# RWKV attention and a routed expert layer in one kernel: products on ScalarE, adds on POOL, routing one step sooner

## The chip, the cores and the metric

The kernel runs on one core of a Trainium2 chip. A core has five engines that run their own instruction streams and meet at semaphores: TensorE (PE in the profile; PEld is its weight load), VectorE (DVE), ScalarE (ACT), GpSimd (POOL), and SyncE (SP), which here only starts transfers. They work on SBUF, 128 partitions of on-chip memory, and PE writes to PSUM, from which the others read. The metric is the device time of one execution in microseconds. The kernel before takes 846.95 us, the median of 3 runs (845.86 to 848.41).

## What is computed

Two layers on x of 4 sequences of 1024 tokens with 256 channels, each added to x. First, on the normalized x, an RWKV attention with 16 heads:

```python
xx = jnp.pad(x, ((0, 0), (1, 0), (0, 0)))[:, :Tv] - x
xk, xv, xr, xg = x + xx*time_maa_k, x + xx*time_maa_v, x + xx*time_maa_r, x + xx*time_maa_g
r, k, v = xr @ Wr.T, xk @ Wk.T, xv @ Wv.T          # per head
g = gelu(xg @ Wg.T)
att = rc @ kc                                      # per chunk of the sequence
yc = att * Wmat @ vc + rc @ state * wb
new_state = ws * state + kc * wk @ vc
yn = (y - mean) / sqrt(var + EPS) * ln_w + ln_b    # per head
out = yn * g @ Wo.T
```

Then, on the normalized result, a layer of 8 experts: each token picks its two likeliest, and each expert takes at most 320 tokens of a sequence, in their order. A token's place comes from a running count:

```python
count_fused = jnp.cumsum(mask_fused, axis=1)
trunc_mask = expert_mask * (count <= capacity)
expert_out = einsum(silu(h1) * h3, w2)             # h1 = dispatch @ w1, h3 = dispatch @ w3
final = einsum('ebcm,bsec->bsm', expert_out, combine_mask)
```

## The kernel before

Phase one (`phase_a`) does the attention and the routing, in 16 blocks of 256 tokens (two tiles of 128; a sequence is four blocks), all in float32. Phase two (`phase_b`) runs the eight experts and isn't touched. Phase one ends with the first part of expert 0 (`early_...`), for which the rows of the first three sequences are enough.

The order on each engine is written out by hand, as a loop over steps c in which each function gets its own block: the same step works on block c+3's statistics, c+1's projections, c's attention, c-1's output, c-2's and c-3's routing. No scheduler moves anything. An engine waits at the first instruction whose semaphore is not up, and all behind it waits too.

In a step PE does, in this order: `scores_a` (L1317), `across` (L1345), `turn1` (L1290, the transposes of normalized x), `project_g`, `outer` (L1308), four `within` of the first tile, `scores_b`, `project_r`, `project_k`, `across`, four `within` of the second tile (L1354, each waits for one mask of DVE), `count(c-3)` (L1401, L1402), `project_o(c-1)` (L1378), `logits` (L1391), `turn_k` (L1298), `group_sums` (L1368), `project_v` (L1275).

The four mixed inputs come from one difference, `diff` (L964 on DVE): inputs 0, 1 and 2 by `mixing` on DVE (L973: product and sum in one instruction, for two halves of the channels), input 3 by `mixed_g` on POOL (two products at L586, one add at L588).

The routing of a block is `logit_sum`, `logit_max` and `stats2` on DVE, `norm2` on POOL (its last result is `nbias`), `logit_exp` on ACT (L745), `best_two` and `tally` on DVE (L1073 to L1093: the two experts and the running sums), `count` on PE, `slots` on DVE (L1100 to L1114: the row number in each expert's list) and `scatter` on POOL (L610: four indirect transfers that write the tokens' rows). `count` writes into the same PSUM bank that `scores_a` uses next; so `scores_a` waits for `slots`.

ACT turns PSUM into SBUF (`turned1` L793, `receptance` L695, `key`, `value`), does the gate (`gate` L806, gT), z (`scaled` L815), the two norms (`normed1` L764, `normed2` L687) and the high part of expert 0's weights (`weight_high` L785), whose low part is formed on POOL (`weight_low` L594). zg, which `project_o` takes, is z times gT on POOL (`gated` L622). The high and low parts need the raw weights, which SP loads with `first_weights` behind the output of blocks 1, 3 and 8.

Of the kernel before, what the change touches and what calls it, by code (L numbers as in the profile page):

```python
# [23 lines left out]
ALU = mybir.AluOpType  # L24
# [265 lines left out]
def phase_a(nc, sb, ps, ctx, sem, ident, x, maa, decay_row, decay_ch, u_row, weights, lnw, lnb, gateT, disp, out,  # L290
# [117 lines left out]
    diff_ready = sem("diff_ready")  # L408
    mixed_ready = [sem(f"mixed_ready{k}") for k in range(4)]
# [49 lines left out]
    def on_sync(sp):  # L459
# [33 lines left out]
        for b in range(STEPS):  # L493
# [4 lines left out]
            if b in (1, 3, 8):  # L498
                first_weights((1, 3, 8).index(b))
# [8 lines left out]
    def on_gpsimd(pool):  # L508
# [70 lines left out]
        def mixed_g(b):  # L579
            if 0 <= b < STEPS:  # L580
                pool.wait_ge(diff_ready, b + 1)
                if b == 0:
                    pool.wait_ge(maa_in, 16)
                wait(pool, proj_done[3], b)
                for k in range(KT):
                    chain.add(nc.gpsimd.tensor_scalar(mixed[3][:, k, :], diff[:, k, :], maa_sb[:, 3, k:k + 1], None, ALU.mult))  # L586
                chain.sync()
                nc.gpsimd.tensor_tensor(mixed[3][:], mixed[3][:], xT[b % 2][:, :, 1:], ALU.add).then_inc(mixed_ready[3], 1)  # L588
# [39 lines left out]
        for c in range(-3, TAIL):  # L628
            norm2(c - 2)
            mixed_g(c + 1)  # L630
            gated(c - 1)
            if c < TAIL - 1:
                scatter(c - 4, range(0, 1))
# [3 lines left out]
            if c < TAIL - 1:  # L637
                scatter(c - 4, range(1, TPS))
            weight_low(c - 6)
            if c >= TAIL - 2:  # L640
                scatter(c - 3)
# [8 lines left out]
        weight_low(9)  # L650
        scatter(12)
        chain.reset()
        norm2(14)
        gated(15)
# [4 lines left out]
        weight_low(11)  # L659
# [5 lines left out]
    def on_scalar(act):  # L665
# [10 lines left out]
        def decay_tables():  # L676
# [3 lines left out]
            nc.scalar.activation(sdecay[:], lam_ch[:], ACT.Exp, scale=-float(Q)).then_inc(set_act, 1)  # L680

# [150 lines left out]
        for c in range(-2, TAIL):  # L832
            group_log(c - 1)
            value(c)
            if c == 0:
                folded()
            turned1(c + 1)
# [3 lines left out]
            normed1(c + 2)  # L841
            scaled(c - 1)
            normed2(c - 2)
# [8 lines left out]
            weight_high(c - 4)  # L852
            keep_y(c)
            column(c + 1)
            keep_logits(c + 1)

# [21 lines left out]
        weight_high(11)  # L878
        early_hidden_hi(2)
        early_gate(3)  # L880
        early_hidden_hi(3)
        logit_exp(15)
        early_gate(4)
        normed2(15)
# [6 lines left out]
    def on_vector(dve):  # L891
# [64 lines left out]
        def shifted(b):  # L956
            if 0 <= b < STEPS:
# [3 lines left out]
                wait(dve, mixed_ready[3], b)  # L961
# [173 lines left out]
        for c in range(-3, TAIL):  # L1135
# [8 lines left out]
            mask(c, 1, 2)  # L1144
            mask(c, 1, 3)
            state_b(c)
            stats1(c + 3)
            if c == -3:
                center_gate()
            mixing(c + 1, 2)  # L1150
# [1013 lines left out]
```

## Time and profile before

| what | us |
| --- | --- |
| median of 3 runs (range) | 846.95 (845.86 to 848.41) |
| the profiled execution | 846.3 |
| its span, first to last instruction | 844.6 |
| PE busy in the span | 814.7 (96%) |
| DVE busy | 505.7 (60%) |
| ACT busy | 464.4 (55%) |
| POOL busy | 468.3 (55%) |
| granted clock of PE, mean | 0.995 of full speed |

The profile comes from one execution. The shares are means over two phases with different limits, so they are read by stretches. In the timeline a line is one instruction or a run of like ones: start, duration to the end of the last, engine, line and operation, what is written and read, how many; in brackets the idle time of the engine before it and what ended it. The ends of matmuls are modelled, and PE's durations overlap; so PE's work is read from one start to the next. A name like L1378 is the line of the kernel before.

### The profile page before, as it was taken

How to read it: one execution, taken by the hardware profiler on the slowest of the kernel's cores; microseconds unless marked ns; L12 is line 12 of the kernel's file. 1: busy time of each engine (PE TensorE's matmuls, PEld its weight loads, DVE VectorE, ACT ScalarE, POOL GpSimd, SP SyncE). 2: the span in 40 equal slices, each digit the busy share in tenths (PEclk: the TensorE clock that was granted, in tenths of full speed). 3: DMA queues.
4: the chain of work that ended last, by engine and by line, in shares of the span. 5: the costliest groups of instructions: out<-in, count | busy, mean ns of one | idle time of the engine just before them, and what ended most of it. 6: DMA issues, size and time to landing. Idle time of an engine off the chain costs nothing. (4 is left out here: it accounts for less than half of the span.)

```text
span 844.6 us, 17509 instructions
## 1 busy us (share of the span) xinstructions
PE 814.7 (96%) x6291; PEld 674.5 (80%) x6291; DVE 505.7 (60%) x1286; ACT 464.4 (55%) x860; POOL 468.3 (55%) x529
## 2 busy tenths in 40 slices
PE   5999999999999989899999999999999999999997
PEld 4777787777777667678998788898788899788886
DVE  6789988899998886343543543544443545353441
ACT  4478877778787667264543543644552544453331
POOL 6445577777777857475444356453436452535215
PEclk9999999999999999999999999999999999999999
DMA  5852032213111121546333334342415442413114
GB/s 163 334 209 70 28 108 68 76 52 96 40 40 48 58 91 72 178 157 135 101 70 40 110 95 70 95 113 27 124 60 79 121 106 26 95 35 44 20 14 50
DMA packets 50746, 74.30 MB, mean 88 GB/s; under 512 B 5072, under 2 KB 42448, under 8 KB 50640
## 3 DMA queue, kind: packets, MB, share of 16 engines
q1 hardware_dynamic: 35760, 53.72, 19.2%
q0 software_dynamic: 14592, 19.18, 13.6%
q8 instruction: 64, 1.05, 0.5%
q14 instruction: 42, 0.34, 0.1%
q10 hardware_dynamic: 288, 0.01, 0.0%
HBM read 38.67 MB, written 34.22 MB: 86 GB/s over the span
## 5 line engine op out<-in xcount | busy, mean ns | idle before, releaser
L1648 POOL DMA_INDIRECT out<-ysb,index x80 | 124.7, 1558 | 145.6 <-DVE ysb L1887 111.1
L2001 PE MATMUL p<-xh,whi 128*128 128x512 f32 (+2 forms) x504 | 185.4, 368 | 1.4 <-POOL wlo L1637 0.5
L1863 DVE TENSOR_TENSOR hid<-gated,p 128x512 f32<-128x512 f32 (+1 forms) x126 | 81.0, 643 | 176.2 <-ACT gated L1710 176.2
L2003 PE MATMUL p<-xh,wlo 128*128 128x512 f32 (+2 forms) x504 | 185.3, 368 | 0.0
L2002 PE MATMUL p<-xl,whi 128*128 128x512 f32 (+2 forms) x504 | 184.6, 366 | 0.0
L2027 PE MATMUL py<-w,hh 128*128 128x512 f32 x448 | 162.5, 403 | 4.2 <-DVE hl L1132 3.7
L1710 ACT ACTIVATE gated<-p 128x512 f32<-128x512 f32 (+1 forms) x126 | 70.8, 562 | 157.4 <-PE p L2003 152.8
L1637 POOL TENSOR_TENSOR wlo<-wraw,whi 128x448 fp32r<-128x448 f32 x56 | 70.8, 1267 | 89.8 <-ACT whi L1696 84.4
L2001 PEld LDWEIGHTS p<-xh,whi 128*128 128x128 f32 x504 | 94.7, 188 | 19.2 <-issue 3.5
L2026 PE MATMUL py<-w,hl 128*128 128x256 f32 x384 | 108.5, 283 | 0.0
L2002 PEld LDWEIGHTS p<-xl,whi 128*128 128x128 f32 x504 | 94.8, 188 | 15.2
L2003 PEld LDWEIGHTS p<-xh,wlo 128*128 128x128 f32 x504 | 94.7, 188 | 14.7
L2027 PEld LDWEIGHTS py<-w,hh 128*128 128x128 f32 x448 | 83.2, 190 | 19.7 <-DVE hl L1132 4.1
L1737 ACT ACTIVATE ysb<-py,weight 128x256 f32<-128x256 f32 x64 | 30.4, 474 | 111.9 <-PE py L2027 90.0
L1871 DVE TENSOR_TENSOR hl<-hid,hh 128x512 fp32r<-128x512 f32 (+1 forms) x126 | 88.9, 706 | 3.8 <-ACT hh L1719 3.3
L1887 DVE SCALAR_TENSOR_TENSOR ysb<-py,weight,ysb 128x256 f32<-128x256 f32 x64 | 30.9, 483 | 99.8 <-ACT ysb L1737 99.8
L992 DVE TENSOR_TENSOR attm<-pS,dmask 128x512 f32<-128x512 f32 x128 | 79.3, 679 | 7.4 <-PE pS L1317 7.0
L610 POOL DMA_INDIRECT disp<-row,slot_i x64 | 65.6, 1025 | 32.4 <-issue 12.0
L2026 PEld LDWEIGHTS py<-w,hl 128*128 128x128 f32 x384 | 72.8, 190 | 2.9
L1719 ACT CAST hh<-hid 128x512 fp32r<-128x512 f32 (+1 forms) x126 | 72.8, 578 | 1.2 <-DVE hid L1863 1.2
L1250 PE MATMUL pB<-mixed,w_in_sb 128*128 128x256 f32 x256 | 61.3, 383 | 0.2 <-ACT gT L806 0.2
L586 POOL TENSOR_SCALAR mixed<-diff,maa_sb 128x256 f32<-128x256 f32 x32 | 37.9, 1192 | 32.3 <-DVE diff L964 32.3
(215 smaller groups left out, 1430.7 us busy)
## 6 DMA issues: line engine op xcount, KB each, us to landing
wraw<-in_w SPq DMA_DIRECT2D x24, 896.0 KB
disp<-wraw SPq DMA_DIRECT2D x16, 662.5 KB, 8.2
xtok<-disp SPq DMA_DIRECT2D x16, 530.0 KB, 4.8
x_ring<-in_x SPq DMA_DIRECT2D x16, 256.0 KB, 3.3
out<-x SPq DMA_DIRECT2D x16, 256.0 KB
xtok<-disp SPq DMA_DIRECT2D x8, 265.0 KB
out<-ysb,index POOLq DMA_INDIRECT x80
disp<-row,slot_i POOLq DMA_INDIRECT x64
```

The costliest lines, as they stand in the source:

```text
L992: nc.vector.tensor_tensor(attm[g][:], pS[:, :, g // 2, g % 2, :], group_mask(g), ALU.mult).then_inc(attm_ready[g], 1)
L1637: nc.gpsimd.tensor_tensor(to.piece(1, m, q), raw_piece(wraw[k], m, q), to.piece(0, m, q).bitcast(F32), ALU.subtract).then_inc(wlo_ready, 1)
L1648: nc.gpsimd.indirect_dma_start(out, bass.IndirectOffsetOnAxis(ap=index[e.const % 2][:, t:t + 1], axis=0), ysb[j % NY][:], None, compute_op ...
L1710: nc.scalar.activation(gated[k][:, 0:w], p1[k][:, 0:w], ACT.Silu).then_inc(gated_ready, 1)
L1719: nc.scalar.copy(hh[(u * NCH + q) % 2][:, f, 0:w], hid[k][:, 0:w]).then_inc(hh_ready, 1)
L1863: nc.vector.tensor_tensor(hid[k][:, 0:w], gated[k][:, 0:w], p3[k][:, 0:w], ALU.mult).then_inc(hid_ready, 1)
L1871: nc.vector.tensor_tensor(hl[s][:, f, 0:w], hid[k][:, 0:w], hh[s][:, f, 0:w].bitcast(F32), ALU.subtract).then_inc(hl_ready, 1)
L2001: nc.tensor.matmul(dst[:, 0:w], hi[m][:, wcut], xh[xcut], start=(kt == 0), stop=False)
L2002: nc.tensor.matmul(dst[:, 0:w], hi[m][:, wcut], xl[xcut], start=False, stop=False)
L2003: ins = nc.tensor.matmul(dst[:, 0:w], lo[m][:, wcut], xh[xcut], start=False, stop=(kt == KT - 1))
L2026: nc.tensor.matmul(to[:, 0:C], b, w2[:, f, 0, :], start=False, stop=False)
L2027: ins = nc.tensor.matmul(to[:], a, w2[:, f].rearrange("p h c -> p (h c)"), start=(f == 0), stop=(f == FT - 1))
```

## The change

- Inputs 2 and 3 are no longer formed by DVE and by POOL alone. ACT forms the products (`mixed_part`: two activations of 128x256 with a scale for each input), and POOL adds x (`mixed_add`).
- A block's routing after `logit_exp` comes one step sooner: `count(c-2)`, `slots(c-2)`, `scatter(c-3)`. `count` stands behind `project_o` on PE, `best_two` and `tally` before `residual` on DVE, `slots` behind `decayed_k`. `stats1` moves behind `stats2`.
- On ACT `normed2` and `normed1` move to the end of the step, `weight_high` comes one step sooner and stands before `turned1`; `weight_low` too comes one step sooner. SP's third weight load goes behind block 7 instead of 8.
- At the end of phase one block 12's `count`, `slots` and `scatter` are gone, the last zg is formed on DVE (`gated_last`), and the last `logit_exp` stands before `early_gate(3)` on ACT.

```diff
         for b in range(STEPS):
...
-            if b in (1, 3, 8):
-                first_weights((1, 3, 8).index(b))
+            if b in (1, 3, 7):
+                first_weights((1, 3, 7).index(b))
...
-        def mixed_g(b):
-            if 0 <= b < STEPS:
-                pool.wait_ge(diff_ready, b + 1)
-                if b == 0:
-                    pool.wait_ge(maa_in, 16)
-                wait(pool, proj_done[3], b)
-                for k in range(KT):
-                    chain.add(nc.gpsimd.tensor_scalar(mixed[3][:, k, :], diff[:, k, :], maa_sb[:, 3, k:k + 1], None, ALU.mult))
-                chain.sync()
-                nc.gpsimd.tensor_tensor(mixed[3][:], mixed[3][:], xT[b % 2][:, :, 1:], ALU.add).then_inc(mixed_ready[3], 1)
+        def mixed_add(b, k):
+            if 0 <= b < STEPS:
+                pool.wait_ge(part_ready[k], b + 1)
+                nc.gpsimd.tensor_tensor(mixed[k][:], mixed[k][:], xT[b % 2][:, :, 1:], ALU.add).then_inc(mixed_ready[k], 1)
...
+        def mixed_part(b, k):
+            if 0 <= b < STEPS:
+                act.wait_ge(diff_ready, b + 1)
+                wait(act, proj_done[k], b)
+                if b == 0:
+                    act.wait_ge(maa_in, 16)
+                for c in range(KT):
+                    ins = nc.scalar.activation(mixed[k][:, c, :], diff[:, c, :], ACT.Copy, scale=maa_sb[:, k, c:c + 1])
+                ins.then_inc(part_ready[k], 1)
...
             value(c)
             if c == 0:
                 folded()
+            weight_high(c - 3)
             turned1(c + 1)
             group_rstd(c - 1)
             logit_exp(c - 2)
             gate(c)
-            normed1(c + 2)
+            mixed_part(c + 1, 2)
+            mixed_part(c + 1, 3)
             scaled(c - 1)
-            normed2(c - 2)
...
             square_y(c)
-            weight_high(c - 4)
             keep_y(c)
             column(c + 1)
+            normed2(c - 2)
             keep_logits(c + 1)
+            normed1(c + 2)
...
+        def gated_last(b):
+            dve.wait_ge(z_ready, b + 1)
+            dve.wait_ge(gT_ready, b + 1)
+            wait(dve, wo_done, b)
+            nc.vector.tensor_tensor(zg[:], z[:], gT[b % 2][:], ALU.mult).then_inc(zg_ready, 1)
...
-                wait(pe, slot_ready, b - 3)
+                wait(pe, slot_ready, b - 2)
...
-            count(c - 3)
             project_o(c - 1)
+            count(c - 2)
```

On POOL the step reads so before (nbias is the end of `norm2`, disp<-row is `scatter`):

```order
L567 TENSOR_TENSOR nbias<-nlmax,rstd 128x2
L586 TENSOR_SCALAR mixed<-diff,maa_sb 128x256 x2
L588 TENSOR_TENSOR mixed<-mixed,xT 128x512
L622 TENSOR_TENSOR zg<-z,gT 128x512
L605 COPY row<-tok 128x2
L610 DMA disp<-row,slot_i 10240x265 x2
L575 TENSOR_TENSOR r_dec<-rT,rdecay 128x512
L610 DMA disp<-row,slot_i 10240x265 x2
```

and so now, in a step with a piece of the weights (the lines are those of the changed kernel):

```order
L568 TENSOR_TENSOR nbias<-nlmax,rstd 128x2
L600 COPY row<-tok 128x2
L605 DMA disp<-row,slot_i 10240x265 x2
L583 TENSOR_TENSOR mixed<-mixed,xT 128x512
L617 TENSOR_TENSOR zg<-z,gT 128x512
L583 TENSOR_TENSOR mixed<-mixed,xT 128x512
L576 TENSOR_TENSOR r_dec<-rT,rdecay 128x512
L605 DMA disp<-row,slot_i 10240x265 x2
L589 TENSOR_TENSOR wlo_0<-wraw,whi_0 128x448
```

The two products are gone, a second add has come, and three operations of 512 elements follow one another between the two pairs of scatters.

On DVE, from the second tile's masks (attm) on, the step reads so before:

```order
L992 TENSOR_TENSOR attm<-pS,dmask 128x512 x4
L1020 SCALAR_TENSOR_TENSOR state<-state,sdecay,kvm 128x32 x2
L950 BN_STATS st<-x_ring 128x6 x2
L953 BN_AGGR mv<-st 128x2 x2
L973 SCALAR_TENSOR_TENSOR mixed<-diff,maa_sb,xT 128x256 x2
L1037 TENSOR_TENSOR x_0<-x_ring,pX 128x256
L1037 TENSOR_TENSOR x_0<-x_ring,pS 128x256
L1047 SCALAR_TENSOR_TENSOR logit<-xg,std_all,pX 128x8
L1047 SCALAR_TENSOR_TENSOR logit<-xg,std_all,pS 128x8
L1100 TENSOR_TENSOR over<-pS,limit 128x16
```

and so now:

```order
L994 TENSOR_TENSOR attm<-pS,dmask 128x512 x4
L1022 SCALAR_TENSOR_TENSOR state<-state,sdecay,kvm 128x32 x2
L1081 TENSOR_REDUCE lsum<-lexp 128x2
L1082 RECIPROCAL lrec<-lsum 128x2
L1083 TENSOR_TENSOR row<-lexp,lrec 128x2x8
L1085 MAX two<-row 128x8 x2
L1087 MEMSET two 128x2x6
L1089 MATCH_REPLACE mark<-two,row 128x8 x2
L1092 TENSOR_SCALAR took<-mark 128x16
L1098 TENSOR_TENSOR before<-before,took 128x8
L1101 TENSOR_TENSOR before<-before,took 128x8
L1045 TENSOR_TENSOR x_0<-x_ring,pX 128x256
```

`best_two` and `tally` (lsum to the second before) now stand between the state's update and `residual` (x_0<-x_ring), where `stats1` and the mix of input 2 stood.

## Rows read from the trace of the kernel before

**Rows 1.** By stretch: its width, busy us (xcount) PE, PEld, DVE, ACT, POOL; PEclk, DMA, GB/s.
```profile
60.00:280.00 220.00, 218.11 (x2686) 171.61 (x2686) 198.12 (x643) 170.13 (x298) 157.84 (x230) 1.00 0.19 63
```

**Rows 2.** Timeline of PE (start us, duration us, engine, line, operation, count): `turn1`.
```profile
59.80 0.66 PE L1290 MATMUL pX<-ident,xn 128*128 128x128 f32 x4
...
77.39 0.66 PE L1290 MATMUL pX<-ident,xn 128*128 128x128 f32 x4
...
95.41 0.66 PE L1290 MATMUL pX<-ident,xn 128*128 128x128 f32 x4
...
187.54 0.66 PE L1290 MATMUL pX<-ident,xn 128*128 128x128 f32 x4
...
279.82 0.66 PE L1290 MATMUL pX<-ident,xn 128*128 128x128 f32 x4
```

**Rows 3.** Timeline of PE: `project_o` and `logits` of one step, `count` of a later one.
```profile
69.73 1.16 PE L1378 MATMUL pX<-w_o,zg 128*128 128x264 f32 x4
...
71.61 0.95 PE L1391 MATMUL pS<-gate_sb,xT 128*128 128x8 f32 x8
...
197.76 0.40 PE L1401 MATMUL pS<-before,ones 128*128 128x16 f32 x2
```

**Rows 4.** Timeline of DVE: first masks of one step, and pieces of a later one.
```profile
59.37 2.48 DVE L992 TENSOR_TENSOR attm<-pS,dmask 128x512 f32<-128x512 f32 x4 [2.40 <-PE pS L1317]
...
193.71 1.24 DVE L1008 SCALAR_TENSOR_TENSOR state<-state,sdecay,kvm 128x32 f32<-128x32 f32 x2
194.88 2.47 DVE L992 TENSOR_TENSOR attm<-pS,dmask 128x512 f32<-128x512 f32 x4
...
197.59 0.74 DVE L950 BATCH_NORM_STATS2 st<-x_ring 128x6 f32<-128x256 f32 x2
...
198.53 0.89 DVE L973 SCALAR_TENSOR_TENSOR mixed<-diff,maa_sb,xT 128x256 f32<-128x256 f32 x2
200.36 0.42 DVE L1037 TENSOR_TENSOR x<-x_ring,pX 128x256 f32<-128x256 f32 x1 [0.94 <-PE pS L1378]
...
203.89 0.16 DVE L1073 TENSOR_REDUCE lsum<-lexp 128x2 f32<-128x16 f32 x1
...
206.17 0.17 DVE L1093 TENSOR_TENSOR before<-before,took 128x8 f32<-128x8 f32 x1
```

**Rows 5.** Timeline of ACT in the same step.
```profile
194.12 1.08 ACT L815 ACTIVATE z<-yn,lnb_sb,lnw_sb 128x256 f32<-128x256 f32 x2
...
196.55 1.26 ACT L704 ACTIVATE r_pair<-pA,parity 128x512 f32<-128x512 f32 x2
```

**Rows 6.** Timeline of POOL in the same step.
```profile
195.28 1.27 POOL L622 TENSOR_TENSOR zg<-z,gT 128x512 f32<-128x512 f32 x1 [0.54 <-ACT z L815]
...
199.95 1.30 POOL L575 TENSOR_TENSOR r_dec<-rT,rdecay 128x512 f32<-128x512 f32 x1
...
203.72 1.15 POOL L594 TENSOR_TENSOR wlo<-wraw,whi 128x448 fp32r<-128x448 f32 x1
```

**Rows 7.** Timeline of DVE: L1075 alone, and beside POOL's L594.
```profile
74.87 0.18 DVE L1075 TENSOR_TENSOR row<-lexp,lrec 128x16 f32<-128x16 f32 x1
...
204.28 0.63 DVE L1075 TENSOR_TENSOR row<-lexp,lrec 128x16 f32<-128x16 f32 x1
```

**Rows 8.** Timeline: first weight's load, ACT's `turned1`; the stretch 79 to 80 us.
```profile
73.53 0.51 SPq L490 DMA_DIRECT2D wraw<-in_w  x1
...
78.08 0.59 ACT L793 COPY xT<-pX 128x512 f32<-128x512 f32 x1 [1.65 <-PE pX L1290]
...
79.00:80.00 1.00, 1.00 (x38) 0.64 (x38) 0.95 (x3) 0.99 (x2) 0.00 (x0) 1.00 0.06 25
```

**Rows 9.** Timeline of PE near the end of phase one: first instructions after waits.
```profile
313.79 1.10 PE L1368 MATMUL pX<-ysq,blockdiag 128*128 128x256 f32 x4 [1.00 <-DVE logit L1047]
...
321.44 1.16 PE L1378 MATMUL pX<-w_o,zg 128*128 128x264 f32 x4 [0.52 <-POOL zg L622]
...
336.07 0.40 PE L1401 MATMUL pS<-before,ones 128*128 128x24 f32 x2 [0.51 <-DVE before L1093]
```

More of the change, by code:

```diff
@@ L408, in phase_a @@
     diff_ready = sem("diff_ready")
+    part_ready = {k: sem(f"part_ready{k}") for k in (2, 3)}
     mixed_ready = [sem(f"mixed_ready{k}") for k in range(4)]
@@ L629, in on_gpsimd @@
             norm2(c - 2)
-            mixed_g(c + 1)
+            scatter(c - 3, range(0, 1))
+            mixed_add(c + 1, 2)
             gated(c - 1)
-            if c < TAIL - 1:
-                scatter(c - 4, range(0, 1))
+            mixed_add(c + 1, 3)
             decayed_r(c + 1)
@@ L636, in on_gpsimd @@
                 empty_rows()
[L637 to L641, printed above, removed]
+            scatter(c - 3, range(1, TPS))
+            weight_low(c - 5)
+            if c == TAIL - 1:
+                scatter(c - 2)
             norm1(c + 3)
@@ L649, in on_gpsimd @@
         weight_low(10)
-        weight_low(9)
-        scatter(12)
-        chain.reset()
+        weight_low(11)
         norm2(14)
-        gated(15)
         scatter(13)
@@ L658, in on_gpsimd @@
         norm2(15)
-        weight_low(11)
         scatter(14)
@@ L877, in on_scalar @@
         early_gate(2)
-        weight_high(11)
         early_hidden_hi(2)
+        logit_exp(15)
         early_gate(3)
+        normed2(15)
         early_hidden_hi(3)
-        logit_exp(15)
         early_gate(4)
-        normed2(15)
         early_hidden_hi(4)
@@ L960, in shifted @@
                 dve.wait_ge(xT_ready, b + 1)
-                wait(dve, mixed_ready[3], b)
+                for k in (2, 3):
+                    wait(dve, mixed_ready[k], b)
                 if b % SPB == 0:
@@ L1146, in on_vector @@
             state_b(c)
-            stats1(c + 3)
+            best_two(c - 2)
+            tally(c - 2)
+            if c < 0:
+                stats1(c + 3)
             if c == -3:
                 center_gate()
-            mixing(c + 1, 2)
             if c == -1:
@@ L1154, in on_vector @@
             logit_sum(c - 1)
-            slots(c - 3)
-            logit_max(c - 1)
-            stats2(c - 1)
             if c == -1:
@@ L1162, in on_vector @@
                 bonus(1)
-            best_two(c - 2)
-            tally(c - 2)
+            slots(c - 2)
+            logit_max(c - 1)
+            stats2(c - 1)
+            if c >= 0:
+                stats1(c + 3)
             mask(c + 1, 0, 0)
@@ L1183, in on_vector @@
         tally(13)
-        slots(12)
-        chain.reset()
         residual(14)
@@ L1194, in on_vector @@
         normed_y(15)
+        gated_last(15)
         best_two(14)
@@ L1202, in on_vector @@
         stats2(15)
+        slots(14)
         chain.reset()
@@ L1206, in on_vector @@
         early_hidden(2)
-        slots(14)
-        chain.reset()
         early_weight()
@@ L1399, in count @@
                 pe.wait_ge(took_ready, b + 1)
-                pe.wait_ge(attm_ready[HGS - 1], min(TPS * b + 8, TPS * STEPS))
+                pe.wait_ge(attm_ready[HGS - 1], min(TPS * b + 6, TPS * STEPS))
                 nc.tensor.matmul(pS[:, 1, 0, 0, 0:n * E], ones[:], before[r][:, 0:n, :].rearrange("p t e -> p (t e)"), start=True, stop=False)
@@ L1476, in on_tensor @@
         within(15, 1, 2)
-        count(12)
         within(15, 1, 3)
@@ L1481, in on_tensor @@
         early_turn(1)
+        count(13)
         group_sums(15)
-        count(13)
         early_up(0)
@@ L1486, in on_tensor @@
         project_o(15)
+        count(14)
         early_up(2)
-        count(14)
         early_up(3)
```

## The prediction, made before the changed kernel ran

> **What bounds the kernel now.** I read the busy times by stretch first. Over 60 to 280 us TensorE (PE) is busy for 218 of 220 us at full clock, VectorE (DVE) for 198, ScalarE (ACT) for 170, POOL for 158 [rows 1]. The change touches only phase one, up to about 343 us; phase two keeps its instructions and counts at nothing.
>
> A busy PE here is PE issuing without a gap, so I measured it by its own rhythm: `turn1` starts once in every step c of the loop, and I call that start T. Between 59.80 and 77.39 us one step takes 17.59 us; the next, with `count` in it, 18.02 [rows 2]. From 77.39 to 279.82 there are eleven steps, 18.40 on average. At 18.02 they would take 4.2 us less: that much waiting stands in the loop, with 0.3 for the step after them 4.5, and no more can be won there.
>
> Where do 0.4 us a step come from? In the step without `count`, `project_o` (L1378) starts at T+9.93; in the one that begins at 187.54, `count` stands in that place and starts at 197.76, T+10.22: the last `within` before it is 0.29 us late, for the fourth mask, which DVE finishes at 197.35 [rows 2 to 4]. DVE goes nearly without a gap from `residual` (200.36) through routing (203.89 to 206.34) and the mixes to the masks of the next step, and `residual` itself waits 0.94 us for PE's `project_o` [rows 4]. PE and DVE hold each other in this loop.
>
> **The change, part by part.** Everything is made against the profiled execution: 846.3 us, of which 1.7 lie outside the span; the median of the three runs is 0.65 us above it.
>
> 1. The routing part (`best_two`, `tally`: 203.89 to 206.34, 2.45 us [rows 4]) leaves DVE's tight stretch for the place before `residual`, where DVE idled; `stats1` (0.94 us, 197.59 to 198.53) goes the other way, and `mixing` of input 2 (0.89 us) goes from that slack place altogether. DVE's tight stretch gets 2.45 - 0.94 = 1.5 us shorter, so the masks are no longer late: minus the 4.5 us, if nothing takes their place.
>
> 2. `count(c-2)` now needs a tally of the same step. On PE `project_o` stays at T+9.93 and takes 1.88 us [rows 3], so that `count` could start at T+11.8. On DVE the second group of masks starts at T+7.34 now [rows 4]. It moves forward by 0.84, since the state updates before it (1.24 us for two, 0.40 without the add of POOL over them) are free; by 0.56, since the first masks start at T-0.43 as at 59.37 and what follows them waits only for PE; and by 0.36, since the mixes have no product of POOL beside them (the last two are estimates). That is T+5.6, and T+8.0 for the end of the masks. `state_b` (0.32) and two small operations bring L1075 to about T+8.67; L1093, 1.89 us later, is done at T+10.7 if nothing holds it. That is in time by a microsecond.
>
> 3. ACT: two products of two pieces each replace nothing on it, and `normed1` and `normed2` move behind. The nearest rows: a 256-wide activation with scale and bias steps at 0.5 us (z, 1.08 for two), a 512-wide one with a scale alone at 0.58 (r_pair, 1.26 for two) [rows 5]. Bounds for a 256-wide one with scale alone: 0.3 and 0.5 us; I take 0.38, between the r_pair row less half its width and the z row. Four are 1.5 us in the place of the 0.99 of `normed1`, so z is ready 0.55 us later than now: T+8.2 instead of T+7.66. POOL then forms zg (1.27 us) to T+9.6, still before PE's T+9.93. At 0.5 us each it would be T+10.0 and cost 0.1 a step.
>
> 4. POOL loses two 256-wide products and gains one 512-wide add. Its order after z is zg, add of input 3, r_dec without a gap: 1.27, about 1.3 and 1.30 less overlaps, from about T+8.3 to T+12.1 [rows 6]. This falls on the routing of point 2. The trace shows what such an operation does to a two-input DVE operation in SBUF: L1075, 16 elements wide, takes 0.18 us alone at 74.87, and 0.63 at 204.28 under POOL's L594 of 203.72, ending 0.04 us after it [rows 6, 7]. The routing has three such operations: L1075, L1090, L1093. L1075 waits for zg, L1090 a little for the add, L1093 comes after r_dec has begun and waits until T+12.1. `count`, at T+11.79 else, starts at about T+12.2: 0.4 us a step, for steps 2 to 5: 1.6 us. (Bounds: nothing, and the full 1.3 of one more such operation.)
>
> 5. From step 5 on the low part of a weight (L594, 1.15 us) follows the second pair of scatters, about T+14.6 to T+15.7. The new place of `slots` has its two-input L1109 at T+15.1: held by some 0.5 us. The statistics behind it, POOL's norms and `logit_exp` slip by up to 0.4 us, and with them z and zg. In such a step r_dec ends at T+12.5, `count` is 0.7 late; or, since L1075 (T+8.67) then stands level with zg (T+8.65), DVE gets through first and the step loses 0.1. Alternating gives 0.25 on average, locked 0.7: I take 0.5, times 9 steps is 4.5 us. The steps behind the ends of sequences have 0.8 us more in `slots`, in the chain to `logit_exp`; `project_k` then waits for gT. 0.7 each, three times: 2.1 us.
>
> 6. `weight_high(0)` comes a step sooner, straight after `value(3)` (about 76.4 us) and ahead of `turned1`. The weight transfer is issued at 73.53 and its last packets move in the window 79 to 80 [rows 8]. `turned1` starts at 78.08 after 1.65 us of waiting for PE; behind a cast of 0.5 us that begins at 79.9 it would be 2.3 us late, of which gate and products take up some, and the earlier `residual` 0.5. One stall of 1.5 us (bounds 0 and 2.5). The third transfer goes a block earlier, behind the same waits: nothing.
>
> 7. The end. One `count` (0.46 us) moves from it into the loop: nothing in sum. Its waits are 1.00 us (group_sums for the logit sum), 0.52 (zg on POOL, now on DVE without the norm before it) and 0.51 (the last `count`) [rows 9]; a longer one for the last hl, at the very end, is a chain of Silu, product, cast and difference after PE's last matmul, and stays. `slots(12)` no longer stands before `residual(14)`, which takes 1.1 us from the first; the second goes. What is late next is ACT: `logit_exp(15)` with two table loads now stands before `early_gate(3)`, and the last tally follows it by DVE's order. I count 1.5 us of the 2.0 as won. Bounds: 0.5 and 3.
>
> 8. The start: block 0's inputs 2 and 3 are formed on ACT while it waits for PE anyway, and DVE is freed: nothing either way (at most 0.5).
>
> Sum: 1.6 + 4.5 + 2.1 + 1.5 = 9.7 added; 4.5 removed; 1.5 won at the end: +3.7. 846.3 + 3.7 = 850.0, and with the 0.65 of the median about **850.6 us**. Own range of this case 848 to 855.
>
> The Trainium skill speaks on point 4. Its page "Advanced Engine Details and Errata", section "VectorE Performance Modes", names as interfering with GPSIMD the Vector instructions that run in a two-port mode, and "VectorE: DVE Perf Modes", in its section on why `tensor_tensor` can't do 2x_2P, keeps two-input operations out of those modes. Taken by the letter, the routing's operations would not be held. The rows of group 7 show the opposite for a two-input operation of 16 elements, and the sum goes by them; by the letter of the page it would be rival B.
>
> **Rivals.**
>
> B, faster: DVE gets through. If L1075, L1090 and L1093 are not held, or only one of them, tally ends before T+11.7 and `count` never waits. For it: with L1075 at T+8.67 and zg at T+8.3 a shift of 0.4 us between ACT and DVE is enough, and the uncertainty of the ACT price is of that size. Against it: the three POOL operations cover 3.8 us and L1075 to L1093 span 1.9. Worked out: 13 steps at 0.05 are 0.7, sequence ends 1.0, point 6 1.5, minus 4.5, minus 2.0 at the end: -3.3, so 843.6.
>
> C, no change: held, but half as long. The DVE operation waiting is let in at each end of a POOL one, and r_dec is pushed behind it: 0.15 in early steps, 0.3 in later ones, 3.3 in all, sequence ends 1.5, point 6 1.0, minus 4.5, minus 1.5: -0.2, so 846.8.
>
> D, clearly slower: ACT becomes the bound. At 0.5 us a product, and with `normed2`, `normed1` and a table load between `keep_y` and `value`, it has 1.2 us of slack left of 18.4; a late `logit_exp` then goes through gate, products, z and zg to `project_o` without a buffer. 0.8 a step over 13 steps is 10.4, ends of sequences 2.0, point 6 2.0, minus 4.5 and 1.0: +8.9, so 855.8.
>
> **How the numbers follow.** Forecast 0.45, B 0.24, C 0.22, D 0.09. A measurement of this kernel can tell about 0.3% (2.5 us, so 844.4 to 849.5) from no change. Slower: forecast and D, 0.54. Same: C, 0.22. Faster: B, 0.24. The range from 842 to 856 holds B and most of D.
>
> **What would show it.** In the changed profile: `within` of the second tile takes 1.0 us, not 1.3; `count`'s first matmul waits for DVE's L1101 (the old L1093) in nearly every step, ending just after POOL's r_dec; the step takes 18.4 to 18.8 us in place of 18.39, and over 19 after the ends of sequences; L1117 is held by the weight's low part; ACT waits for a DMA once, near 77 us; the waits at the end are gone but for hl. I am wrong if steps take 18.1 us or less with L1098 and L1101 at 0.17 us each (then B), or if `project_o` waits for zg and not `count` for tally (then D).

## The result, and the profile after

The changed kernel takes 854.9 us (median of 4 runs, 854.46 to 856.18) against 846.4 (4 runs, 845.1 to 848.41): 1.0105 of the time before, with a 95% interval of 1.0089 to 1.0121. It is slower, as forecast, but by 8.5 us and not by 3.7. (Ratios, here and below, leave out a run that lies more than 1.5% above the fastest of its kernel; medians are of all runs.) The profiled execution is 855.07 us with a span of 853.3, so 8.7 us more than the span of before.

Where are they? T is again the start of `turn1`. Timeline of PE of the changed kernel, one step, with what ended a wait in brackets:

```profile
213.93 0.66 PE L1298 MATMUL pX<-ident,xn 128*128 128x128 f32 x4
...
221.07 1.97 PE L1258 MATMUL pB<-mixed,w_in_sb 128*128 128x256 f32 x8 [0.46 <-ACT gT L806]
...
224.96 1.16 PE L1386 MATMUL pX<-w_o,zg 128*128 128x264 f32 x4 [0.34 <-POOL zg L617]
...
227.67 0.40 PE L1409 MATMUL pS<-before,ones 128*128 128x16 f32 x2 [0.66 <-DVE before L1101]
```

The next `turn1` starts at 233.83: this step takes 19.90 us. In it PE waits in three places, for gT, for zg and for the tally. The twelve steps from 59.61 to 292.02 take 232.4 us; the twelve of before, 59.80 to 279.82 [rows 2], took 220.0. So the loop lost 12.4 us. From the last `turn1` to the first matmul of phase two (343.55 before, 352.21 after) it is 60.2 us in place of 63.7: the end won 3.5. Another 0.2 was won at the start, and 12.4 less 3.5 less 0.2 is the whole 8.7.

By stretch (columns as in [rows 1]): PE is busy for 95% of the loop where it was 99%, ACT works 20 us more (its new products), DVE 13 more although the mix of input 2 was taken from it.

```profile
59.60:292.00 232.40, 220.78 (x2692) 170.21 (x2688) 211.00 (x631) 190.49 (x348) 162.29 (x232) 1.00 0.19 62
```

Waits of the changed kernel from 60 to 292 us (who, for whom: total us, times, longest):

```profile
ACT lexp L745 <- POOL nbias L568: 9.9, 10, 1.2
...
PEld pX L1386 <- POOL zg L617: 6.4, 11, 0.6
...
PE pS L1409 <- DVE before L1101: 5.6, 12, 0.7
...
PE pX L1386 <- POOL zg L617: 3.5, 11, 0.4
...
PE pB L1258 <- ACT gT L806: 2.3, 5, 0.5
```

PE's three waits come to 11.4 us, nearly the 12.4 that the loop lost. The first line, nbias, was not there before, so I followed it back. POOL in the same step, then ACT:

```profile
213.93 0.24 POOL L551 TENSOR_SCALAR nmean<-mv 128x2 f32<-128x2 f32 x1 [3.02 <-issue]
...
215.78 0.22 POOL L551 TENSOR_SCALAR nmean<-mv 128x2 f32<-128x2 f32 x1
...
217.87 0.44 POOL L568 TENSOR_TENSOR nbias<-nlmax,rstd 128x2 f32<-128x2 f32 x1
...
222.56 1.12 POOL L583 TENSOR_TENSOR mixed<-mixed,xT 128x512 f32<-128x512 f32 x1
223.61 1.30 POOL L617 TENSOR_TENSOR zg<-z,gT 128x512 f32<-128x512 f32 x1
224.85 1.10 POOL L583 TENSOR_TENSOR mixed<-mixed,xT 128x512 f32<-128x512 f32 x1
225.90 1.28 POOL L576 TENSOR_TENSOR r_dec<-rT,rdecay 128x512 f32<-128x512 f32 x1
```

```profile
218.34 0.68 ACT L745 ACTIVATE lexp<-logit,nbias,rstd 128x8 f32<-128x8 f32 x2 [1.19 <-POOL nbias L568]
...
220.33 0.60 ACT L806 ACTIVATE gT<-pB 128x512 f32<-128x512 f32 x1
220.83 1.70 ACT L679 ACTIVATE mixed<-diff,maa_sb 128x256 f32<-128x256 f32 x4
222.42 1.08 ACT L815 ACTIVATE z<-yn,lnb_sb,lnw_sb 128x256 f32<-128x256 f32 x2
```

POOL is idle for 3.02 us and then begins `norm1(c+3)` (213.93), whose input `stats1` DVE now forms last of all, up to T; only behind it comes `norm2` (215.78), whose input had been ready since T-1.1. nbias is there at T+4.4. Before the change (timelines of POOL and of ACT there) both norms stood in the same order, but they began 1 us ahead of T, so that nbias was there at T+2.6, 0.5 us before `logit_exp`:

```profile
186.56 0.23 POOL L550 TENSOR_SCALAR nmean<-mv 128x2 f32<-128x2 f32 x1
...
189.96 0.20 POOL L567 TENSOR_TENSOR nbias<-nlmax,rstd 128x2 f32<-128x2 f32 x1
```

```profile
190.67 0.66 ACT L745 ACTIVATE lexp<-logit,nbias,rstd 128x8 f32<-128x8 f32 x2
```

Of the 1.8 us by which nbias is later, 1.0 is the later start of the norms. The other 0.8 is that two of POOL's own small operations behind it take longer than before: the `var` of `norm2` 0.74 us in place of 0.22, nbias 0.44 in place of 0.20.

Late by 1.3 us is then everything behind `logit_exp` on ACT: gT, products, z. POOL is late in its own queue as well: the norms hold up the first two scatters, and the first add starts (222.56) as the second of them ends. So POOL's series of four 512-wide operations (add, zg, add, r_dec), which stands at T+6.6 to T+11.9 in the step from 59.61, where nbias is early, slides onto T+8.6 to T+13.2. There DVE is at the second state update and the routing. Timeline of DVE in that step, and both kernels' views of one line of source (ns: least/median/most), after and then before:

```profile
221.89 3.08 DVE L1022 SCALAR_TENSOR_TENSOR state<-state,sdecay,kvm 128x32 f32<-128x32 f32 x2
...
225.28 0.71 DVE L1083 TENSOR_TENSOR row<-lexp,lrec 128x16 f32<-128x16 f32 x1
...
227.45 0.17 DVE L1101 TENSOR_TENSOR before<-before,took 128x8 f32<-128x8 f32 x1
```

```profile
L1022 DVE SCALAR_TENSOR_TENSOR state<-state,sdecay,kvm x18: 236/1298/1862, 67.6 to 281.5; 128x32 f32<-128x32 f32 x18
```

```profile
L1020 DVE SCALAR_TENSOR_TENSOR state<-state,sdecay,kvm x18: 232/236/243, 68.7 to 271.4; 128x32 f32<-128x32 f32 x18
```

The state update, 32 elements wide with two inputs in SBUF, takes 1.3 us in the median in place of 0.24; in the step shown the two take 3.08 us in place of 0.40. The tally is done at T+13.7, `residual` and the statistics follow it, and with them the next nbias: the loop closes on itself.

### The profile page after: what moved, and what is told of

Same layout as the page of the kernel before. It is cut to its first block and busy times, and to the rows that moved or that the text cites. A ratio compares the mean times of both kernels' runs of the same rounds, so it can differ in the third digit from the quotient of the medians.

```text
span 853.3 us, 17550 instructions
## 1 busy us (share of the span) xinstructions
PE 814.7 (95%) x6291; PEld 671.6 (79%) x6291; DVE 516.0 (60%) x1255; ACT 489.8 (57%) x924; POOL 458.4 (54%) x512
## 3 DMA queue, kind: packets, MB, share of 16 engines
q1 hardware_dynamic: 35760, 53.72, 19.3%
q8 instruction: 64, 1.05, 0.5%
## 5 line engine op out<-in xcount | busy, mean ns | idle before, releaser
L605 POOL DMA_INDIRECT disp<-row,slot_i x64 | 66.7, 1043 | 33.2 <-POOL row L600 12.1
L1258 PEld LDWEIGHTS pB<-mixed,w_in_sb 128*128 128x128 f32 x256 | 46.9, 192 | 12.0 <-issue 6.5
```

The costliest lines, as they stand in the source:

```text
L1258: ins = nc.tensor.matmul(dst[:, m, :], w_in_sb[k][:, c, m * P:(m + 1) * P], mixed[k][:, c, :], start=(c == 0), stop=(c == KT - 1))
```

## The experiments

All are compared with the kernel before, run on the same chip beside them. E1 to E4 ran together, E5 to E8, E9 to E12, and E13 to E15. The kernel before had medians of 847.0, 847.5, 845.9 and 846.7 us in these four groups; in the first, two of its 19 runs were far out (909 and 2039 us). Each reading of a trace is of one execution.

**E1: the second norm first.** In POOL's loop:

```
-            norm2(c - 2)            # head of the step
             ...
+            norm2(c - 1)            # end of the step, ahead of
             norm1(c + 3)
```

> The changed kernel with one thing moved: POOL forms the second norm of a block (norm2, which ends in nbias) before the first norm of a later block (norm1) and not behind it. Theory N (late nbias): since stats1 went behind stats2 on VectorE, norm1 stands in front of norm2 on POOL and makes nbias 1.5 to 2 us late (T+3.9 to T+4.4 in place of T+2.4), logit_exp with it by 0.6 to 1.3 us, and everything behind it on ScalarE. Then nbias comes at T+2.3, logit_exp starts at T+3.1 without a wait, steps take 18.3 to 18.5 us and the kernel about 843 us (841 to 846). Theory H (POOL's operations hold the small VectorE operations, as the prediction had it): tally and slots stay late, steps stay at 18.9 or more, 851 to 854 us. Theory D (ScalarE's products are the bound): the wait for nbias goes, but steps stay above 19, 852 us or more.

Measured: 844.79 us (10 runs, 843.73 to 845.45), 0.9976 of before (0.9967 to 0.9986), 10 us under the changed kernel. Steps of 18.34, as theory N said. nbias and `logit_exp`, 2.5 us apart (POOL, then ACT), state_b, and PE's largest wait:

```profile
189.44 0.20 POOL L568 TENSOR_TENSOR nbias<-nlmax,rstd 128x2 f32<-128x2 f32 x1
```

```profile
192.10 0.66 ACT L744 ACTIVATE lexp<-logit,nbias,rstd 128x8 f32<-128x8 f32 x2
```

```profile
L1021 DVE SCALAR_TENSOR_TENSOR state<-state,sdecay,kvm x20: 234/239/247, 68.3 to 288.8; 128x32 f32<-128x32 f32 x20
```

```profile
PE pS L1408 <- DVE before L1100: 2.5, 12, 0.3
```

The twelve steps take 220.4 us, so 12.0 of the 12.4 us are gone with one change of order on POOL: given the two halves of the change, `norm1` ahead of `norm2` is the cause. It does not make the loop faster than before (220.0). What is left is `count`'s wait for the tally, since L1097 is held to the end of r_dec at T+11.9: 0.2 to 0.3 us a step.

**E2: count later.** In PE's loop of the changed kernel:

```
-            count(c - 2)
             logits(c + 1)
+            count(c - 2)
```

> The changed kernel with count(c-2) behind logits(c+1) on TensorE and not ahead of it, so that TensorE needs the tally 1 us later. Theory N (late nbias is the first cause, count's wait for the tally adds to it): count's waits (0.3 to 0.7 us a step) go, k_dec and slots come as much sooner, and some of the wait for nbias with them; steps of 18.6 to 19.2, 845 to 850 us. If the wait of count for the tally were the whole of the loss, steps would be back at 18.4 or less and the kernel at 844 or less. If it lay beside other work, nothing would change: 854 to 855.

Measured: 860.74 us (859.62 to 861.15), 1.0167 (1.0145 to 1.0188): worse than the changed kernel, against every branch. `count` waits no more, but the wait for nbias grew:

```profile
ACT lexp L745 <- POOL nbias L568: 18.4, 10, 2.6
PE pB L1258 <- ACT gT L806: 11.2, 9, 1.9
```

Work that arrives sooner on DVE now meets POOL's weight_low: the last two-input operation of `slots` ran from T+16.9 to T+18.0, under it, where in the changed kernel it began at T+16.8 just as weight_low ended. Its 1 us lies before the statistics, so nbias comes later still. Here, to take away a wait that is a consequence won nothing.

**E3: both moves.**

> Both moves together: norm2 before norm1 on POOL, and count behind logits on TensorE. Theory N with the tally's wait as second cause: neither wait is left, steps of 17.9 to 18.2, 837 to 842 us, below both kernels. Theory H: slots and masks still late, 848 or more. Theory D: ScalarE's chain (products, z, zg) still sets project_o, 850 or more.

Measured: ten runs from 839.6 to 862.6, median 855.0, which is 1.009 of the 847.0 of before; the ratio on record, 1.0006 (0.997 to 1.0042), leaves out the upper six of the ten. The profiled one, 839.59, is the fastest. It shows the steps hoped for (17.93) but one of 19.06, in which state_b began at T+8.4, as zg did, took 2.3 us for 0.4, and the tally was late. The six runs from 853.0 up have a mean granted clock of 0.981 to 0.988, the four others 0.990 to 0.998. That they hold steps like those of E4 and E11 is likely and not shown: no trace of one was kept. The expectation held for the best executions alone.

**E4: r_dec later.** E1, and in POOL's loop:

```
-            decayed_r(c + 1)
             scatter(c - 3, range(1, TPS))
+            decayed_r(c + 1)
```

> norm2 before norm1 on POOL, and decayed_r on POOL behind the scatters of the second tile, so that no 512-wide POOL operation runs beside the end of the tally. It tests the hold: if POOL's r_dec keeps VectorE's two-input operations L1098 and L1101 waiting (T+12.1 as in the step from 59.6 us), they are now 0.17 to 0.2 us each, the tally ends at T+11.0 to T+11.5 and count waits for nothing: 0.2 to 0.4 us a step less than with norm2 first alone, 838 to 842 us. If the operations are late for another reason, the time is that of norm2 first alone.

Measured: 857.59 us (852.96 to 867.63), 1.0115 (1.0064 to 1.0166) without the slowest. In seven of the twelve steps the hold was gone as expected: L1097 and L1100 0.2 us each, tally at T+11.1, no wait, 17.9 us for most. But two steps took 25.1 and 23.9 us. The same steps came in E11, where they are read.

**E5: stats1 back.** On DVE of the changed kernel, in every step:

```
             state_b(c)
+            stats1(c + 3)
             best_two(c - 2)
             ...
-            stats1(c + 3)
             mask(c + 1, 0, 0)
```

> The changed kernel with stats1(c+3) on VectorE back ahead of the routing (behind state_b) in every step, and POOL's order as changed. It takes away what made norm1, and so norm2 behind it, late, in another way than moving norm2. Theory N (late nbias, then POOL's block of 512-wide operations slides onto state_b and the routing): nbias at about T+2.4, logit_exp at T+3.1, state_b 0.24 us each, steps 18.3 to 18.4, 843 to 846 us. If the order on POOL, and not the late stats1, were the cause: 850 or more. If stats1 ahead of the routing pushes the tally: count waits 0.5 to 0.9 longer, 849 to 855.

Measured: 884.56 us (879.61 to 885.74), 1.0416 (1.0383 to 1.045). nbias was early and `logit_exp` never waited for it, but `stats1` pushed the routing by 1 us onto POOL's series; tallies came at T+15 to T+16 in every second step, and PE stood for it, up to 2.6 us at once, with a lower granted clock behind it (0.64 over the 9.5 us after 154.7; steps of about 19 and of 23 to 26 us in turn). Theory N had forecast 843 to 846 here, so an early nbias is not enough by itself, and this run neither adds to E1 nor speaks against it: the old place of `stats1` was not free for the new order.

**E6: routing alone.** The changed kernel with inputs 2 and 3 formed as before (ACT, DVE, POOL):

```
-            mixed_part(c + 1, 2); mixed_part(c + 1, 3)
+            normed1(c + 2)          # and normed2(c - 2) behind scaled
             state_b(c)
+            mixing(c + 1, 2)
             best_two(c - 2)
-            mixed_add(c + 1, 2); ...; mixed_add(c + 1, 3)
+            mixed_g(c + 1)
```

> The changed kernel without its first half: input 2 is formed by VectorE again (between state_b and the routing) and input 3 by POOL alone, with normed1 and normed2 on ScalarE at their old places; the routing one step sooner, stats1 last and the end of phase one stay. Theory N: nbias is still late (norm1 ahead of norm2, stats1 last), 3.9 us or later, but ScalarE's chain to z is 0.55 us shorter and no add stands between z and r_dec, so less falls on state_b and the routing: 847 to 852 us. If the products are harmless the time is that of the changed kernel, 854 to 856; if they are the whole cause, 844 or less.

Measured: 856.06 us (854.8, 855.8, 856.3 and one of 887.1), 1.0093 (1.0073 to 1.0114) for the first three. `logit_exp` waits 17.2 us in all for nbias, PE 9.7 for gT. Six of the twelve steps take 19.6 us, five 18.2 to 18.6; the first takes 20.97, with one wait of 1.15 us for the tally and a granted clock of 0.71 to 0.86 in the 8 us behind it. The late nbias is a matter of the routing half. The time is over the 847 to 852 that theory N gave.

**E7: products alone.** The kernel before with this (ACT, DVE, POOL):

```
-            normed1(c + 2)
+            mixed_part(c + 1, 2); mixed_part(c + 1, 3)
-            mixing(c + 1, 2)
-            mixed_g(c + 1)
+            mixed_add(c + 1, 2)
             gated(c - 1)
+            mixed_add(c + 1, 3)
```

> The kernel before with only the products moved: ScalarE forms them for inputs 2 and 3, POOL adds, normed2 and normed1 go behind column and keep_logits; routing, stats1, count and the end of phase one as before. Theory N: stats1 is early, nbias comes at T+2.4, and the routing lies in the next stretch, away from POOL's block; VectorE has 0.9 us less work, so the masks are less late: steps 18.0 to 18.4, 842 to 847 us. Theory D (ScalarE's longer chain is the bound): project_o waits for zg, steps 18.8 or more, 850 us or more.

Measured: 858.47 us (857.87 to 859.14), 1.0131 (1.0114 to 1.0148). I expected a gain. Steps equal those of before (17.59, 18.02) until POOL's scatters begin, and are 19.3 to 20.1 from then on. Here nbias is hardly waited for (0.9 us in all); it is POOL's operations again. r_dec stands behind the first pair of scatters and moved from T+12.4 to T+14.3, onto `slots` (POOL, then DVE); the two steps before the first weight_low already take 19.57 and 19.31 us. weight_low moved from T+16.2 to T+18.1, onto the routing:

```profile
167.48 1.30 POOL L576 TENSOR_TENSOR r_dec<-rT,rdecay 128x512 f32<-128x512 f32 x1
```

```profile
167.80 1.02 DVE L1118 TENSOR_TENSOR slotf<-slotf,took 128x16 f32<-128x16 f32 x1
```

So the halves cost 0.9% and 1.3% singly, and 1.05% together. In the changed kernel the first scatters stand ahead of the adds and the routing lies elsewhere, so this loss of the products' half is not there; it has the late nbias in its place.

**E8: the state update ahead of the masks.** E3, and on DVE:

```
             state_a(c)
+            state_b(c)
             mask(c, 1, 0)
             ...
-            state_b(c)
```

> norm2 before norm1 on POOL, count behind logits on TensorE, and state_b(c) on VectorE directly behind state_a(c), ahead of the masks of the second tile. In the runs with the first two moves alone state_b started at T+8.1, some 0.2 us before POOL's zg; where it started at T+8.5 it was held for 2.3 us instead of 0.4, the tally came 3 us late and TensorE stood still. Theory of the hold: with state_b at about T+5.7 nothing two-input stands near zg, every execution takes 837 to 841 us, and none is above 845. If the slow executions come from something else, they are still there, with a median above 845.

Measured: ten runs of 841.8 to 853.4, median 848.06, 1.0002 (0.9972 to 1.0032): narrower than E3, not as narrow as expected. In its profile an operation of 16 elements took 3.45 us in two steps, and ended with the last of three of POOL's (DVE, then POOL):

```profile
141.21 3.45 DVE L1082 TENSOR_TENSOR row<-lexp,lrec 128x16 f32<-128x16 f32 x1
```

```profile
141.06 1.30 POOL L617 TENSOR_TENSOR zg<-z,gT 128x512 f32<-128x512 f32 x1
142.30 1.10 POOL L583 TENSOR_TENSOR mixed<-mixed,xT 128x512 f32<-128x512 f32 x1
143.34 1.27 POOL L576 TENSOR_TENSOR r_dec<-rT,rdecay 128x512 f32<-128x512 f32 x1
```

`count` waited 0.98 us for it in each, and in the 7.2 us behind the wait the granted clock was 0.76: both steps take 21.1 us, where most of the others take 17.9 to 18.1.

**E9: that move alone**, on the changed kernel.

> The changed kernel with one thing moved: state_b(c) on VectorE directly behind state_a(c), ahead of the masks of the second tile; nbias stays late. In the changed kernel state_b's operations take 1.3 us in the median in place of 0.24, since POOL's adds and zg have slid onto them. Theory of the hold with the late nbias as its cause: logit_exp still waits to T+4 or later, but 1 to 2.5 us of holding go from the way to the tally; steps of 18.7 to 19.2, 848 to 852 us. If the holding of state_b lay beside other waits: 854 to 856.

Measured: 859.85 us (858.47 to 862.35), 1.0159 (1.0142 to 1.0176). Wrong as E2 was, and for the same reason: state_b was no longer held, but the wait for nbias rose to 14.8 us and `slots` met weight_low.

**E10: E8 with a shorter series.** POOL's order:

```
             gated(c - 1)
-            mixed_add(c + 1, 3)
             decayed_r(c + 1)
             scatter(c - 3, range(1, TPS))
+            mixed_add(c + 1, 3)
```

> The kernel of e8_state_early (norm2 before norm1, count behind logits, state_b ahead of the masks) with POOL's add of input 3 behind the scatters of the second tile. In e8 one 16-wide operation of the routing (the product of lexp and lrec) took 3.45 us where zg, that add and r_dec ran without a gap beside it. Without the add the longest cover is 2.5 us, and usually zg alone. Theory of the hold: the tally ends by T+12.4 in every step, steps 17.9 to 18.1, 837 to 842 us in nearly every execution. If executions above 845 are still the half, the scatter of times has another source than the cover of these three.

Measured: 841.47 us (840.25 to 844.24), 0.9958 (0.9941 to 0.9975): faster than both kernels. Eight of the twelve steps from 59.4 us take 17.9 to 18.1; PE's waits are down to 0.8 us in all.

**E11: the shorter series without the two other moves** (E1 and the late add).

> norm2 before norm1 on POOL and POOL's add of input 3 behind the scatters of the second tile; count stays ahead of logits, state_b behind the masks. Theory of the hold: r_dec then ends at T+10.9 and not T+11.9, the tally at about T+11.3 to T+11.5, count waits for nothing, and steps take 17.9 to 18.1 in place of 18.34: 839 to 843 us, if masks and state_b stay ahead of zg; where they slip by 0.3 us single steps cost 1 to 3 more. If the tally is not late for r_dec, 844 to 845 as with norm2 first alone.

Measured: 866.3, 867.0, 870.6 and 846.6 us. Beside it the kernel before took 845.9, so the expected gain did not come. Half the steps of the profiled run (866.3) take 17.9 to 18.1 us as expected, three take 23 to 26. PE of one of them, and the stretches before, in and behind the wait:

```profile
185.29 0.39 PE L1408 MATMUL pS<-before,ones 128*128 128x16 f32 x2 [3.88 <-DVE before L1100]
...
189.76 3.46 PE L1282 MATMUL pA<-w_in_sb,mixed 128*128 128x256 f32 x8
```

```profile
169.00:181.00 12.00, 11.89 (x176) 9.30 (x168) 11.93 (x24) 10.98 (x21) 10.18 (x16) 1.00 0.07 25
181.00:185.30 4.30, 0.42 (x3) 0.01 (x1) 3.99 (x13) 0.70 (x2) 3.89 (x4) 1.00 0.18 63
185.30:194.80 9.50, 9.50 (x61) 7.56 (x61) 4.97 (x21) 4.18 (x7) 3.07 (x11) 0.64 0.49 153
```

state_b took 3.44 us for two, and ended with the last of three of POOL's operations. L1100 took 2.74: it began half a microsecond into a scatter and ended with the add and the weight_low behind it. PE waited 3.88 us, and in the next 9.5 us its granted clock was 0.64 of 2.4 GHz, so mostly 1.2: `project_v` took 3.46 us, where it takes 1.89 at full clock. A late tally costs its wait and, where PE stood for 3.9 us, about 3.4 us of clock (9.5 less 0.64 of it) on top.

**E12: products alone, r_dec ahead of the scatters.** E7, and on POOL:

```
+            decayed_r(c + 1)
             scatter(c - 4, range(0, 1))
-            decayed_r(c + 1)
```

> The kernel with the products moved alone (858 us: r_dec at T+14.3 to T+15.6 holds slots, the low part of the weight at T+18.1 holds the routing) with r_dec on POOL ahead of the first tile's scatters, so that it runs at about T+11 to T+12.3, where VectorE has residual with one operand in PSUM. Theory of the hold: slots' operation takes 0.17 us, k_dec and the routing come about 1 us sooner, steps of 18.3 to 18.9, 846 to 852 us. If the loss came from ScalarE's longer chain instead, 857 to 859.

Measured: 863.41 us (862.78 to 864.45), 1.0209 (1.0192 to 1.0226). `slots` was free again, as said, but weight_low now came behind all four scatters, past T, and the norms behind it: `logit_exp` waits 14.8 us for nbias. So the forecast gain did not come, and neither of the two places tried for r_dec is free.

**E13: both adds late.** E10, with `mixed_add(c + 1, 2)` moved to stand ahead of `mixed_add(c + 1, 3)`.

> The kernel of e10_add_late_all with both of POOL's adds behind the scatters of the second tile, so that zg and r_dec alone stand beside the masks' end and the routing. In e10 the product of lexp and lrec took 2.4 us in two steps (from 131.9 and 204.3 us: 18.43 in place of 17.93), where the add of input 2 came late (T+7.7) and pushed zg. Theory of the hold: these two steps take 17.9 to 18.1, about 1 us less in all: 839 to 842 us, and no execution above 844. If input 2 comes too late for project_v, TensorE waits in every step and the time is 845 or more.

Measured: 858.1 us (858.02 to 860.23), 1.0138 (1.0121 to 1.0155). The routing had less over it, as said, but the adds and weight_low formed a new series at T+13.3 to T+16.6, over `slots` (DVE, then POOL):

```profile
157.88 1.86 DVE L1116 TENSOR_TENSOR slotf<-slotf,took 128x16 f32<-128x16 f32 x1
```

```profile
156.44 2.17 POOL L583 TENSOR_TENSOR mixed<-mixed,xT 128x512 f32<-128x512 f32 x2
158.53 1.17 POOL L589 TENSOR_TENSOR wlo<-wraw,whi 128x448 fp32r<-128x448 f32 x1
```

`scores` waits for `slots`, 8.5 us in all, and most steps take 19.0 us. project_v, which I had named as the risk, waited once for 0.2 us, its weight loads for 3.5 in all.

**E14: E10 with the first weight transfer a block sooner** (`if b in (0, 3, 7)` in place of `(1, 3, 7)`).

> The kernel of e10_add_late_all with the first weight transfer issued by the sync engine after block 0 and not after block 1. It tests the one stall of point 6: ScalarE's weight_high(0) waits about 2 us for the transfer near 77 us. If that is worth what the step shows (18.68 against 17.93 us), the kernel is 0.7 us faster than e10, 840 to 841.5 us; if the transfer disturbs the loads of the next blocks, it is slower.

Measured: 841.45 us (840.3 to 842.51), 0.9937 (0.992 to 0.9954), E10's time. The intervals of the two ratios overlap. The stall is gone (17.87 in place of 18.68 us), but five steps of 18.4 to 18.7 stand where E10 has two besides the stall. The 0.7 us can't be told.

**E15: E10 with count ahead of logits,** as the changed kernel has it.

> The kernel of e10_add_late_all with count(c-2) ahead of logits again. It tells apart which of two moves keeps away the steps of 24 to 25 us that came with the add late alone (tally at T+16, TensorE idle for some 4 us, its clock granted at half in the next 10 us). If state_b ahead of the masks does, 840 to 844 us here too. If count's place does (1.4 us of slack for a late tally), there are executions of 850 or more.

Measured: 844.24 us (ten runs, 840.5 to 850.4), 0.9978 (0.9949 to 1.0007), one of ten at 850 and five above 845. So neither branch holds as written. There is no step of 24 us in its profile (a run of 842.96), which speaks for state_b's place as what keeps those away, but one trace does not show it for the slower runs. Three steps of 19.05, where L1082 was held to T+11.3 and `count` waited, show what count's later place is worth: with the same hold E10's steps take 18.43.

## Why the prediction was right and wrong

The side and the range held; the size did not (+8.5 for +3.7). By place: with the `count` that moves into it, the loop was forecast to lose about 5.7 us and lost 12.4; the end was forecast to win 2.0 and won 3.5. That the time lies in the range is in part these two errors taking from each other.

- Point 1 is the step that failed. It booked the move of `stats1` as 0.94 us of DVE and stopped there. Its consumer `norm1` stands ahead of `norm2` in POOL's queue, so the move delays nbias by 1.8 us where the slack was 0.5. E1 shows that this alone is worth 10 us. The masks came when the forecast said (the second group at T+5.6, done at T+8.0), but the 4.5 us of waiting were not won in the changed kernel, and in E1 `count`'s wait took their place (220.4 us for the twelve steps, 220.0 before). The loop wins only where steps take 17.93 us, as in the profiled runs of E3 and E10: 217.3 and 217.5 us.
- Point 2: `state_b` was counted at 0.32 and the tally at T+10.7 unhindered. Unhindered that is right: in steps of E2 where neither is held it was done at T+10.5 (in E4's undisturbed steps at T+11.1, with L1082 still under zg). That state_b itself would be held was not seen; it is the largest single hold (3.08 us for two in place of 0.40).
- Point 3 was right: four products step by 0.40 us (497 ns each, overlapped), z at T+8.3 where `logit_exp` was not late, zg at T+9.6, `project_o` without a wait. The Trainium skill gives the same in "ScalarE: Activation LUTs", section "What ACT_TABLE_LOAD costs": 186 ns, 0.833 an element and 93 for a pointer make an estimate of 492 ns, with an overlap of 93; the trace agrees.
- Point 4, the hold of the routing, is right in mechanism and, in steps with an early nbias, in size: E1's tally ends at T+12.1, as forecast, and `count` starts at T+12.2; only the operation held to the end of r_dec is the first of the two, not L1100. `count` waited 5.6 us in all in the changed kernel.
- Point 5 (0.5 us for nine steps, 2.1 for the ends of sequences, 6.6 us) has the chain from `slots` over norms and `logit_exp` to z, but with a slip of 0.4 us from weight_low as its cause. That hold of `slots` came in two steps of the changed kernel (0.56 us for 0.17); `logit_exp` was 0.9 to 1.3 late in ten, from the norms.
- Point 6: 1.8 us of waiting for the transfer near 77 us, as said; with nothing else late it makes that step 0.3 (E1) to 0.75 us (E10) longer, not 1.5.
- Point 7: the end won 3.5 us, not 1.5. In E1, with an early nbias, 2.2 (61.5 us from the last `turn1` to phase two, against 63.7). The rest may be lateness of the loop that the end makes up; no run isolates it. One wait there that was to be gone is new: PE waits 2.0 us for DVE's `hid` at 341.32.
- Rival D gave nearly the time (855.8), by luck: its cause, ACT as the bound, is wrong, since ACT's price was 0.40 and not 0.5 and E1 with the same products takes 844.8. The path that it drew behind a late `logit_exp`, over gT, z and zg to `project_o`, is what happened; PE waited for zg and for the tally, 0.34 and 0.66 us in one step, so both signs were there, that of the forecast and that of D. Rival B's "not held" is refuted by state_b's 1.3 us and by E1's L1097, 1.19 us in place of 0.17. The page that it leaned on is corrected by another of the Trainium skill, "SBUF — State Buffer", section "SBUF: two separate sides": of a DVE operation with two SBUF inputs and a GpSimd one that reads SBUF, the one that starts first blocks the other for its whole length. The trace agrees, and adds that the wait can outlast several of POOL's operations.

What stays open: which of two waiting engines gets in between two operations that follow without a gap. The routing's product (L1083, L1082 in E8) got in behind zg in some steps and sat through three in others; no run isolates why. Nor was a slow run of E3, E8 or E15, whose runs lie 10 to 23 us apart, looked at beside a fast one. Clear of the kernel before, on the fast side, are E1 (0.2%), E10 (0.4%) and E14 (0.6%). Of the gain of E10's profiled run, 6.5 us under the span of before, 2.5 us lie in the twelve steps and 2.4 between the last `turn1` and phase two; no edit separates the two.

## What to carry to other kernels

When a step moves on one engine, follow its result into the queue of the next engine and ask who stands behind it there: a norm that nobody was in a hurry for held back the one that closed the loop, and its slack of 0.5 us could be read off the trace before. When a loop is closed through several engines, remove the first lateness and not the waits that it causes; E2 and E9 took away a consequence and were slower. Long series of wide POOL operations want a place where VectorE has one operand in PSUM: `residual` takes 0.42 us beside r_dec (199.95 and 200.36 before, [rows 4, 6]), as it does in all 16 blocks. And a series is worse than its operations apart: three without a gap held one small operation for 3.45 us.

## What was not expected of the hardware

- A VectorE operation of 16 elements took 3.45 us beside three POOL operations without a gap (E8), and two of 32 elements 3.44 us (E11), where 0.18 and 0.40 is the time alone.
- It seems to go both ways: POOL's nbias, 2 elements wide, takes 0.20 us alone and 0.44 at 217.87 beside DVE's operations, and in E6 up to 1.04.
- Behind a wait of 3.88 us PE was granted 0.64 of its clock for 9.5 us (E11); behind waits of 0.66 the granted clock stayed at 1.00 (the changed kernel). In E5, 0.75 over 6.7 us soon after one of 1.44. The shortest wait with a loss behind it is 0.98 us (E8: 0.76 over 7.2 us, so some 1.7 us lost), but behind one of 1.30 (E5, 222.65) the clock stayed at 1.00 for 6.2 us. The length of the wait alone does not decide it.
